# The second edge sweep's sums kept feature by node, on top of the node's own row, and read as they are by the output layer

## The chip, the cores and the metric

One core of a Trainium2 chip runs the whole program in one launch. The metric is the device time of an execution in microseconds; the kernel before takes 1228.67 us (median of 3 runs, 1228.24 to 1230.1).

## The reference

The program computes two graph layers with a residual and a layer norm behind each. There are 1250 nodes with 512 features and 20000 edges, sorted by one end. All of it is fp32.

```python
x = layernorm(x + attention_layer(x))               # first sweep over the edges
# second layer
pre = irrep_linear(x)                               # p0 (128) and p1 (3 x 128)
s0  = [p0[dst], p0[dst], sum_m p1[dst]*p1[src]/3]
g   = silu([x0, |x1|] @ W_g1 + b_g1) @ W_g2 + b_g2
x'  = irrep_linear([g0, x1*g1])                     # the node's own row, 512 wide
w1..w4 = (ssp(edge_attr @ W_f1) @ W_f2) * (ssp(s0 @ W_s1) @ W_s2)
out0 = w1*x0'[src]*sh0 + w4*sum_m x1'[src]*sh1/sqrt(3)
out1 = w2*x0'[src]*sh1 + w3*x1'[src]*sh0
out  = segment_sum([out0, out1], dst) + x'          # sums over edges, plus the own row
out  = [out0 @ W_o0 + b_o0, out1 @ W_o1]            # output layer, per 128-wide part
x    = layernorm(x + out + x)
```

## The kernel before, in words

The nodes are padded to 1280 and stand in `NB` = 10 blocks of `P` = 128. The edges are sorted into `NG` = 88 groups of 256 slots; a group belongs to one block of nodes and is worked on as two halves of 128 edges (`k` = 0, 1). Every engine runs its own instruction list in the order in which `pipelined` (L565) and its short form `pairs` (L584) call the steps: a step with lag n does in iteration i the work of group (or pair of blocks) i - n. Nothing reorders them. Semaphores join the engines. Each `nc.Block()` is a stage; all engines meet at its end.

The stages are: sorting the edges and loading them into slots; the first sweep (L590 on); the node stage (L763 on), which takes the ten blocks in five pairs; the second sweep (L1001 on), 88 groups; and the output stage (L1246 on), again five pairs of blocks.

**The node stage.** For a pair q, VectorE makes the normed row `x1c` (`residual`, `norm`), TensorE turns it (`turn_x`, L888) into PSUM `psX`, ScalarE copies that to `xT` (`x_out`, L841). From `xT` come the squares (`squares`, L803 to L807), `pre` (L896, L899), the gate (`gate1` L906 and L907, `gate_hidden` L859, `gate2` L922, `gate_out` L869, `gated` L820) and the new row (`new_x`, L929 and L931). VectorE's `table_row` (L828, L829) writes it to `tabrow`, raises `row_ready`, and SyncE stores `tabrow` to the table in DRAM that the second sweep gathers from. `keep_self` (L875) is a ScalarE copy of `tabrow` into `selfx`. After the last pair's `residual`, GpSimd clears the accumulator `acc` (L951).

**The second sweep.** For each half k of a group, VectorE has made the messages `mm_sb` (edges on the partitions, 768 wide: 512 for the own components, then 128 and 128 more), a one-hot `oh` of the target node, and `ohs[.., 0..3, :]`, the one-hot scaled by each of the four spherical components (ScalarE makes 1 to 3). TensorE's `sums` adds them up in the PSUM bank `psA`. The one-hot is the stationary operand and the messages move, so `psA` is node by feature:

```python
pe.matmul(psA, ohs[:, u, k, 0, :], mm_sb[:, u, k, 0:D], start=(k == 0), stop=False)      # 512 columns
for m in range(3):                                                                       # 3 x 128 columns
    pe.matmul(psA[:, P*(m+1):P*(m+2)], ohs[:, u, k, m+1, :], mm_sb[:, u, k, D:D+P], start=False, stop=False)
mm = pe.matmul(psA[:, 0:P], oh[:, u, k, :], mm_sb[:, u, k, D+P:D+2*P], start=False, stop=(k == 1))
```

VectorE's `accumulate` (L1197) adds `psA` to the block's rows of `acc`. TensorE's order in one iteration is `inner` (L1055), `sums(0)`, `hidden` (L1082, L1084), `sums(1)`, `sources` (L1096), `factors` (L1109).

**The output stage.** For a pair q: GpSimd adds `acc` and `selfx` into `ya` (`with_self`, L1304); TensorE turns `ya` (`turn_sums`, L1314) into `psY`; ScalarE copies it to `yT` (`sums_out`, L1290); TensorE multiplies it by `W_o0` and `W_o1` into `psO` (`layer`, L1322); VectorE makes the residual `hb` (`residuals`, L1253 and L1255), adds `psO` (`add_layer`, L1260 and L1263), takes the statistics (L1268, L1273), ScalarE the square root (L1294), VectorE the reciprocal and the normed row (`norm`, L1278 and L1282), and SyncE stores it (L1331). `psO` has one buffer: `layer(q)` waits until `add_layer(q - 1)` is done.

Of the kernel before, what the change touches and what calls it, by code (L numbers as in the profile page):

```python
# [8 lines left out]
ALU = mybir.AluOpType  # L9
# [5 lines left out]
P = 128  # L15
# [26 lines left out]
def build(nc, x, src, dst, edge_rows, W, b, a, W_pre0, b_pre0, W_pre1, W_nd0, b_nd0, W_nd1, W_g1, b_g1,  # L42
          W_g2, b_g2, W_f1, W_f2, W_s1, W_s2, W_o0, b_o0, W_o1, out):
    ctx = ExitStack()
    with ctx:
# [710 lines left out]
        xn_ready = sem("xn_ready")  # L756
        row_ready = sem("row_ready")
        self_ready = sem("self_ready")
        tab_out = sem("tab_out")
# [3 lines left out]
        with nc.Block() as block:  # L763
# [69 lines left out]
            def _(act):  # L833
# [38 lines left out]
                def keep_self(q):  # L872

                    act.wait_ge(row_ready, q + 1)
                    act.activation(selfx[:, bass.ds(q * 2, 2), :], tabrow[:, :, 0:D], ACT.Copy).then_inc(self_ready, 1)  # L875
                pairs(act, (1, lengths), (1, p0_out), (1, gate_hidden), (2, keep_self), (0, deviation), (1, part_out),
# [3 lines left out]
            def _(pe):  # L880
                def turn_x(q):

                    pe.wait_ge(x1_ready, q + 1)
                    after(pe, xT_ready, q)
                    for c in range(4):
                        for k in range(2):
                            s_ = x1c[:, k, 0:P] if c == 0 else x1c[:, k, P + c - 1:D:3]
                            mm = pe.transpose(psX[:, c // 2, GE * (c % 2) + P * k:GE * (c % 2) + P * k + P], s_, ident[:, :])  # L888
                    mm.then_inc(xtr_ready, 1)
# [35 lines left out]
                def new_x(q):  # L925
# [6 lines left out]
                    mm.then_inc(xn_ready, 1)  # L932
                pairs(pe, (1, pre), (1, gate1), (1, part), (1, gate2), (0, turn_x), (1, new_x))

# [8 lines left out]
            @block.gpsimd  # L943
            def _(gp):
                def keep_x1(q):
                    gp.wait_ge(x1_ready, q + 1)
                    gp.tensor_copy(x1[:, bass.ds(q * 2, 2), :], x1c[:, :, :]).then_inc(x1_copied, 1)
                pairs(gp, (0, keep_x1))

                gp.wait_ge(hb_ready, NB // 2)  # L950
                gp.memset(acc[:, :, :], 0.0)  # L951

# [48 lines left out]
        with nc.Block() as block:  # L1001
# [45 lines left out]
            def _(pe):  # L1047
# [11 lines left out]
                def sums(k):  # L1059
                    def step(g, c, n):  # L1060
                        u = c % 2
                        if k == 0:
# [3 lines left out]
                            after(pe, acc2_done, g)  # L1066
                        pe.matmul(psA, ohs[:, u, k, 0, :], mm_sb[:, u, k, 0:D], start=(k == 0), stop=False)  # L1067
                        for m in range(3):
                            pe.matmul(psA[:, P * (m + 1):P * (m + 2)], ohs[:, u, k, m + 1, :], mm_sb[:, u, k, D:D + P],  # L1069
                                      start=False, stop=False)  # L1070
                        mm = pe.matmul(psA[:, 0:P], oh[:, u, k, :], mm_sb[:, u, k, D + P:D + 2 * P], start=False, stop=(k == 1))  # L1071
                        if k == 1:
# [150 lines left out]
        sweep2.close()  # L1223
        ya = sb("ya2", [P, 2, D])
        yT = sb("yT2", [P, 2, D])
        hb = sb("hb2", [P, 2, D])
# [4 lines left out]
        outrow = sb("outrow", [P, 2, D])  # L1231
        oa_ready = sem("oa_ready")
        oaT_ready = sem("oaT_ready")
        oT_ready = sem("oT_ready")
        ow_ready = sem("ow_ready")
# [8 lines left out]

        psY, psO = ps[:, 0:2, :], ps[:, 2:4, :]
        with nc.Block() as block:  # L1246
# [40 lines left out]
            def _(act):  # L1287
                def sums_out(q):
                    act.wait_ge(oaT_ready, q + 1)
                    act.activation(yT[:, :, :], psY, ACT.Copy).then_inc(oT_ready, 1)  # L1290

                def deviation(q):
                    act.wait_ge(omv_ready, q + 1)
                    act.activation(sd_[:, :], mv[:, :, 1], ACT.Sqrt, bias=epsc[:, 0:1]).then_inc(osd_ready, 1)  # L1294
                act.preload_act_table_set("sqrt_and_others")
                pairs(act, (0, sums_out), (1, deviation))

            @block.gpsimd
            def _(gp):
                def with_self(q):  # L1300

                    two = bass.ds(q * 2, 2)
                    after(gp, oaT_ready, q)
                    gp.tensor_tensor(ya[:, :, :], acc[:, two, 0:D], selfx[:, two, :], ALU.add).then_inc(oa_ready, 1)  # L1304
                pairs(gp, (0, with_self))

            @block.tensor
            def _(pe):
                def turn_sums(q):
                    pe.wait_ge(oa_ready, q + 1)  # L1310
                    after(pe, oT_ready, q)
                    for k in range(2):
                        for c in range(4):
                            mm = pe.transpose(psY[:, k, P * c:P * c + P], ya[:, k, P * c:P * c + P], ident[:, :])  # L1314
                    mm.then_inc(oaT_ready, 1)

                def layer(q):
                    pe.wait_ge(oT_ready, q + 1)
                    after(pe, oh_done, q)
                    for k in range(2):  # L1320
                        for c in range(4):
                            mm = pe.matmul(psO[:, k, P * c:P * c + P], yT[:, k, P * c:P * c + P],  # L1322
                                           (wo1 if c else wo0)[:, :], start=True, stop=True)
                    mm.then_inc(ow_ready, 1)
                pairs(pe, (0, turn_sums), (0, layer))

# [33 lines left out]
```

## Time and profile before

| | |
|---|---|
| median of 3 runs | 1228.67 us (1228.24 to 1230.1) |
| the profiled execution's own time | 1229.83 us |
| its span in the trace | 1228.1 us |
| TensorE (matmul) busy | 995.1 us, 81% of the span |
| VectorE busy | 854.4 us, 70% |
| GpSimd busy | 780.0 us, 64% |
| ScalarE busy | 533.3 us, 43% |
| node stage | from about 469 to 550 us of the span |
| second sweep | from about 550 to 1185 us |
| output stage | from about 1185 us to the end |

The busy time of TensorE comes from matmuls whose ends are modelled; where one follows another, the start to start distance tells what it costs. An fp32 matmul stands in the trace as two instructions of the same size, each with a weight load of its own; a transpose of an fp32 tile as one. A row of the timeline may merge several equal instructions in a row (x6) into one. The granted clock of TensorE is given as a share of 2.4 GHz, so 0.50 is 1.2 GHz.

### The profile page before, as it was taken

To read this page: it belongs to the slowest core of one execution; us is meant where nothing else is said; L and a number is where in the kernel's file an instruction comes from. 1 tells how busy PE (TensorE), PEld (TensorE's weight loads), DVE (VectorE), ACT (ScalarE), POOL (GpSimd) and SP (SyncE) were. 2 spreads that over 40 slices of the span, in tenths; PEclk is the share of its full clock that TensorE was granted. 3 is DMA by queue.
4 is the path that set the end of the run, shared out by engine and by line. 5 is a ranking of instruction groups with operands and counts; after the bars stand their busy time and mean duration, and the time that the engine had idled before them with its cause. 6 is when DMAs were issued, how large, how long until landed. Compare 5 with 4: busy or idle time off the path is not lost. (4 is left out here: it accounts for less than half of the span.)

```text
span 1228.1 us, 23671 instructions
## 1 busy us (share of the span) xinstructions
PE 995.1 (81%) x5530; PEld 642.5 (52%) x5531; DVE 854.4 (70%) x2190; ACT 533.3 (43%) x1559; POOL 780.0 (64%) x809
## 2 busy tenths in 40 slices
PE   2316556199999996756999999999999999999974
PEld 1213232055555554643666666666666666666653
DVE  7351101177778775744888888888888888888857
ACT  2203121023222333543665666656566555666631
POOL 3777777577777760116676776767667676676721
PEclk9757668699999997886999999999999999999987
DMA  9201011277877780125545545455454555545302
GB/s 346 76 15 33 25 32 50 75 238 238 242 240 241 240 218 17 60 94 180 171 156 165 163 153 171 150 167 161 157 170 148 170 159 159 166 150 167 127 1 86
DMA packets 109167, 177.46 MB, mean 145 GB/s; under 512 B 40191, under 2 KB 79343, under 8 KB 109009
## 3 DMA queue, kind: packets, MB, share of 16 engines
q0 software_dynamic: 33184, 130.15, 33.5%
q1 hardware_dynamic: 72752, 45.60, 12.4%
q10 hardware_dynamic: 3200, 1.38, 0.5%
q8 instruction: 11, 0.18, 0.1%
q14 instruction: 20, 0.16, 0.0%
HBM read 157.31 MB, written 19.74 MB: 144 GB/s over the span
## 5 line engine op out<-in xcount | busy, mean ns | idle before, releaser
L1038 POOL TENSOR_TENSOR dot<-ring,ed 128x768 f32<-128x768 f32 x88 | 129.6, 1473 | 134.1 <-issue 109.8
L698 PE MATMUL ps<-ring,aw 128*128 128x512 f32 x352 | 195.6, 643 | 17.7 <-DVE aw L649 16.3
L1028 POOL DMA_INDIRECT ring<-tab_d,ed x176 | 170.4, 968 | 62.2 <-issue 30.5
L618 POOL DMA_INDIRECT ring<-xt_d,ed x176 | 167.5, 952 | 61.4 <-issue 42.0
L375 POOL DMA_INDIRECT slots_d<-stage,stage_pos x157 | 153.5, 978 | 66.3 <-issue 48.7
L1067 PE MATMUL ps<-mm_sb,ohs 128*128 128x512 f32 x352 | 189.1, 619 | 1.4 <-DVE acc L1197 1.4
L1069 PEld LDWEIGHTS ps<-mm_sb,ohs 128*128 128x128 f32 x1056 | 145.6, 191 | 84.2 <-issue 84.2
L1122 ACT ACTIVATE ohs<-oh,ed 128x128 f32<-128x128 f32 x528 | 172.6, 394 | 0.0
L1152 ACT ACTIVATE S_sb<-ps 128x512 f32<-128x512 f32 x176 | 95.5, 595 | 134.6 <-PE ps L1109 134.6
L1069 PE MATMUL ps<-mm_sb,ohs 128*128 128x128 f32 x1056 | 146.2, 275 | 0.0
L1175 DVE TENSOR_TENSOR ps<-S_sb,ps 128x1024 f32<-128x1024 f32 x88 | 108.2, 1229 | 28.0 <-ACT S_sb L1152 26.8
L699 PEld LDWEIGHTS ps<-ring,aw 128*128 128x128 f32 x352 | 67.5, 192 | 85.7 <-issue 85.7
L1055 PEld LDWEIGHTS ps<-ident,prod 128*128 128x128 f32 x528 | 57.1, 142 | 86.2 <-DVE prod L1165 76.1
L1109 PE MATMUL ps<-w,hcat 32*128 32x512 f32 x704 | 101.3, 645 | 0.8 <-DVE hcat L1170 0.8
L1197 DVE TENSOR_TENSOR acc<-acc,ps 128x512 f32 x88 | 60.6, 688 | 45.7 <-PE ps L1071 45.7
L661 DVE TENSOR_TENSOR acc<-acc,ps 128x513 f32 x88 | 60.7, 690 | 43.1 <-issue 30.1
L1055 PE MATMUL ps<-ident,prod 128*128 128x128 f32 x528 | 78.0, 285 | 13.3 <-DVE prod L1165 12.0
L1165 DVE TENSOR_TENSOR prod<-ps,ring 128x768 f32<-128x768 f32 x88 | 83.6, 950 | 6.8 <-DMA ring<-tab_d,ed 6.8
L1185 DVE TENSOR_TENSOR mm_sb<-ps,ring 128x768 f32<-128x768 f32 x88 | 83.3, 946 | 0.0
L1096 PE MATMUL ps<-p1h,ohT 128*128 x176 | 67.7, 385 | 10.3 <-DVE ohT L1216 10.0
L284 DVE CAST stage<-loc_i 128x16 f32<-128x16 int32 (+1 forms) x10 | 1.8, 182 | 105.0 <-DMA slots_d<-stage,stage_pos 104.9
L630 DVE SCALAR_TENSOR_TENSOR junk<-iota,ed,srow 128x128 f32<-128x128 f32 x176 | 54.9, 348 | 24.7 <-DMA ed<-slots_d 18.5
(194 smaller groups left out, 1859.0 us busy)
## 6 DMA issues: line engine op xcount, KB each, us to landing
ilb<-f_d SPq DMA_DIRECT2D x88, 128.0 KB, 3.8
ed<-slots_d SPq DMA_DIRECT2D x176, 38.0 KB, 3.8
tab_d<-tabrow SPq DMA_DIRECT2D x5, 896.0 KB, 3.7
slots_d<-fill SPq DMA_DIRECT2D x8, 418.0 KB, 4.3
f_d<-ft SPq DMA_DIRECT2D x88, 38.0 KB
ring<-xt_d,ed POOLq DMA_INDIRECT x176, 4.0
hcat<-f_d SPq DMA_DIRECT2D x176, 16.0 KB, 3.8
ring<-tab_d,ed POOLq DMA_INDIRECT x176, 4.4
```

Source lines behind the costliest of these rows:

```text
L375: g.indirect_dma_start(slots_d[:, :], bass.IndirectOffsetOnAxis(ap=stage_pos[:, h, k:k + 1], axis=0), stage[:, h, k, :], None).then_inc(sc ...
L618: gp.indirect_dma_start(xg[:, c, k, :], None, xt_d[:, :], bass.IndirectOffsetOnAxis(ap=ed[:, c, k, JD:JD + 1].bitcast(I32), axis=0))\
L698: pe.matmul(ps[:, 2 * u, :], aw[:, r, k, :], xg[:, c, k, 0:D], start=(k == 0), stop=(k == 1))
L1028: gp.indirect_dma_start(xj[:, r, k, :], None, tab_d[:, :], bass.IndirectOffsetOnAxis(ap=ed[:, c, k, JD:JD + 1].bitcast(I32), axis=0))\
L1038: gp.tensor_tensor(dot[:, u, :, :, :], xj[:, r, :, P:D].rearrange("p k (m n) -> p k m n", m=3), ed[:, c, :, IL + 2:IL + 5].unsqueeze(3).to ...
L1055: mm = pe.matmul(psI[:, P * k:P * k + P], prod[:, k, P * m:P * m + P], ident[:, :], is_transpose=True, start=(m == 0), stop=(m == 2))
L1067: pe.matmul(psA, ohs[:, u, k, 0, :], mm_sb[:, u, k, 0:D], start=(k == 0), stop=False)
L1069: pe.matmul(psA[:, P * (m + 1):P * (m + 2)], ohs[:, u, k, m + 1, :], mm_sb[:, u, k, D:D + P], start=False, stop=False)
L1109: mm = pe.matmul((psS if q < 2 else psF)[:, q % 2, :], hcat[rows, c, :], w2[rows, :], start=True, stop=True)
L1122: ins = act.activation(ohs[:, u, k, m, :], oh[:, u, k, :], ACT.Copy, scale=ed[:, c, k, IL + 1 + m:IL + 2 + m])
L1152: ins = act.activation(S_sb[:, k, :], psS[:, k, :], ACT.Copy)
L1175: v.tensor_tensor(psF, S_sb[:, :, :], psF, ALU.mult).then_inc(w_done, 1)
```

## The change

In the second sweep, the messages become the stationary operand and the one-hots move, so that `psA`, and with it `acc`, are feature by node within each block of 128 by 128. For one half of a group the 512-wide matmul becomes four of 128 columns (one for each 128 features), and the three of 128 columns that shared the message part `mm_sb[.., D:D+P]` become one of 384 columns. In the node stage TensorE turns the new row (`turn_self`) into `psX` as soon as it is in `tabrow`, and ScalarE's `keep_self` copies it from there into `acc`, rearranged, in place of the copy into `selfx`; GpSimd no longer clears `acc`. `psX` is shared with `turn_x`, which now waits for `keep_self` of the pair that was turned before. In the output stage the GpSimd addition, the turn and the ScalarE copy are gone, and `layer` takes `acc` as its stationary operand.

```diff
@@ node stage
                 def keep_self(q):
-                    act.wait_ge(row_ready, q + 1)
-                    act.activation(selfx[:, bass.ds(q * 2, 2), :], tabrow[:, :, 0:D], ACT.Copy).then_inc(self_ready, 1)
+                    act.wait_ge(self_turned, q + 1)
+                    act.activation(acc[:, bass.ds(q * 2, 2), 0:D].rearrange("p k (c n) -> p c k n", n=P),
+                                   psX.rearrange("p a b -> p (a b)").rearrange("p (c k n) -> p c k n", c=4, k=2), ACT.Copy).then_inc(self_ready, 1)
@@
                     pe.wait_ge(x1_ready, q + 1)
                     after(pe, xT_ready, q)
+                    after(pe, self_ready, q - 1)
                     for c in range(4):
@@
-                pairs(pe, (1, pre), (1, gate1), (1, part), (1, gate2), (0, turn_x), (1, new_x))
+
+                def turn_self(q):
+
+                    pe.wait_ge(row_ready, q + 1)
+                    for c in range(4):
+                        for k in range(2):
+                            mm = pe.transpose(psX[:, c // 2, GE * (c % 2) + P * k:GE * (c % 2) + P * k + P],
+                                              tabrow[:, k, P * c:P * c + P], ident[:, :])
+                    mm.then_inc(self_turned, 1)
+                pairs(pe, (1, pre), (2, turn_self), (1, gate1), (1, part), (1, gate2), (0, turn_x), (1, new_x))
@@
                 pairs(gp, (0, keep_x1))
-
-                gp.wait_ge(hb_ready, NB // 2)
-                gp.memset(acc[:, :, :], 0.0)
@@ second sweep
-                        pe.matmul(psA, ohs[:, u, k, 0, :], mm_sb[:, u, k, 0:D], start=(k == 0), stop=False)
-                        for m in range(3):
-                            pe.matmul(psA[:, P * (m + 1):P * (m + 2)], ohs[:, u, k, m + 1, :], mm_sb[:, u, k, D:D + P],
-                                      start=False, stop=False)
-                        mm = pe.matmul(psA[:, 0:P], oh[:, u, k, :], mm_sb[:, u, k, D + P:D + 2 * P], start=False, stop=(k == 1))
+                        for m in range(4):
+                            pe.matmul(psA[:, P * m:P * m + P], mm_sb[:, u, k, P * m:P * m + P], ohs[:, u, k, 0, :],
+                                      start=(k == 0 and m == 0), stop=False)
+                        pe.matmul(psA[:, P:D], mm_sb[:, u, k, D:D + P], ohs[:, u, k, 1:4, :].rearrange("p m n -> p (m n)"), start=False, stop=False)
+                        mm = pe.matmul(psA[:, 0:P], mm_sb[:, u, k, D + P:D + 2 * P], oh[:, u, k, :], start=False, stop=(k == 1))
@@ output stage
-        psY, psO = ps[:, 0:2, :], ps[:, 2:4, :]
+        psO = ps[:, 0:2, :]
@@ scalar
-                def sums_out(q):
-                    act.wait_ge(oaT_ready, q + 1)
-                    act.activation(yT[:, :, :], psY, ACT.Copy).then_inc(oT_ready, 1)
...
-                pairs(act, (0, sums_out), (1, deviation))
-
-            @block.gpsimd
-            def _(gp):
-                def with_self(q):
-
-                    two = bass.ds(q * 2, 2)
-                    after(gp, oaT_ready, q)
-                    gp.tensor_tensor(ya[:, :, :], acc[:, two, 0:D], selfx[:, two, :], ALU.add).then_inc(oa_ready, 1)
-                pairs(gp, (0, with_self))
+                pairs(act, (0, deviation))
@@ tensor
-                def turn_sums(q):
-                    pe.wait_ge(oa_ready, q + 1)
-                    after(pe, oT_ready, q)
-                    for k in range(2):
-                        for c in range(4):
-                            mm = pe.transpose(psY[:, k, P * c:P * c + P], ya[:, k, P * c:P * c + P], ident[:, :])
-                    mm.then_inc(oaT_ready, 1)
-
                 def layer(q):
-                    pe.wait_ge(oT_ready, q + 1)
                     after(pe, oh_done, q)
                     for k in range(2):
                         for c in range(4):
-                            mm = pe.matmul(psO[:, k, P * c:P * c + P], yT[:, k, P * c:P * c + P],
+                            mm = pe.matmul(psO[:, k, P * c:P * c + P],
+                                           acc[:, q * 2 + k, P * c:P * c + P],
                                            (wo1 if c else wo0)[:, :], start=True, stop=True)
                     mm.then_inc(ow_ready, 1)
-                pairs(pe, (0, turn_sums), (0, layer))
+                for q in range(NB // 2):
+                    layer(q)
```

TensorE's list in the loop of the node stage, before (`x1c` is the normed row, `xT` the turned one, `n1T` the lengths, `hT` the hidden gate):

```order
L896 MATMUL ps<-xT,wpre 128x256
L899 MATMUL ps<-wpre,xT 128x128 x6
L906 MATMUL ps<-xT,wg 128x256
L907 MATMUL ps<-n1T,wg 128x256
...
L914 MATMUL ps<-ws1ab,p0T 128x32 x2
L922 MATMUL ps<-hT,wg 128x256 x4
...
L888 MATMUL ps<-ident,x1c 128x128 x8
```

And with the change, where L899, L902, L909, L910, L917, L925 and L891 are the same steps under their new line numbers:

```order
L899 MATMUL ps<-xT,wpre 128x256
L902 MATMUL ps<-wpre,xT 128x128 x6
L942 MATMUL ps<-ident,tabrow 128x128 x8
L909 MATMUL ps<-xT,wg 128x256
L910 MATMUL ps<-n1T,wg 128x256
...
L917 MATMUL ps<-ws1ab,p0T 128x32 x2
L925 MATMUL ps<-hT,wg 128x256 x4
...
L891 MATMUL ps<-ident,x1c 128x128 x8
```

The eight transposes of the row from two iterations back (L942) now stand between `pre` and `gate1`, so `gate1` and all behind it on TensorE are queued behind their wait for `row_ready`.

## Rows read from the trace of the kernel before

**Rows 1.** Windows by stage: busy us of each engine (instructions), granted clock share, DMA
```profile
700.00:900.00 200.00, 197.91 (x1320) 130.45 (x1319) 175.13 (x345) 120.93 (x373) 139.12 (x143) 1.00 0.51 162
...
1185.00:1228.10 43.10, 20.68 (x120) 19.11 (x120) 28.71 (x60) 7.88 (x11) 11.15 (x5) 0.72 0.16 62
```

**Rows 2.** Timeline of TensorE, second sweep, one group: start us, us busy
```profile
800.56 1.02 PE L1067 MATMUL ps<-mm_sb,ohs 128*128 128x512 f32 x2
801.42 0.83 PE L1069 MATMUL ps<-mm_sb,ohs 128*128 128x128 f32 x6
802.09 0.39 PE L1071 MATMUL ps<-mm_sb,oh 128*128 128x128 f32 x2
...
802.97 1.12 PE L1067 MATMUL ps<-mm_sb,ohs 128*128 128x512 f32 x2
...
807.49 1.02 PE L1067 MATMUL ps<-mm_sb,ohs 128*128 128x512 f32 x2
```

**Rows 3.** Line L1067 over the whole run: weight loads (ns), idle before them (us, times)
```profile
L1067 PEld LDWEIGHTS ps<-mm_sb,ohs x352: 186/190/192, 577.4 to 1182.1; 128*128 128x128 f32 x176
...
  issue: 17.8, 87
```

**Rows 4.** Timeline, node stage, from one normed row to the next
```profile
489.12 1.13 PE L888 MATMUL ps<-ident,x1c 128*128 128x128 f32 x8 [1.37 <-DVE x1c L797]
...
494.00 0.60 PE L906 MATMUL ps<-xT,wg 128*128 128x256 f32 x2
494.09 0.41 DVE L829 TENSOR_TENSOR tabrow<-ps,bnd_bc 128x256 f32<-128x256 f32 x1
...
495.99 0.84 ACT L859 ACTIVATE hT<-ps,bg 128x256 f32<-128x256 f32 x2
...
496.71 1.05 ACT L875 ACTIVATE xt<-tabrow 128x1024 f32 x1
...
497.79 1.28 ACT L836 ACT_TABLE_LOAD   x1
...
500.19 0.29 ACT L836 ACTIVATE sd_<-mv,epsc 128x2 f32<-128x2 f32 x1 [1.11 <-DVE mv L786]
...
501.77 1.97 PE L888 MATMUL ps<-ident,x1c 128*128 128x128 f32 x8 [2.90 <-DVE x1c L797]
```

**Rows 5.** Timeline, end of the node stage and first rows of the next
```profile
534.59 0.41 DVE L829 TENSOR_TENSOR tabrow<-ps,bnd_bc 128x256 f32<-128x256 f32 x1
534.70 0.30 PEld L906 LDWEIGHTS ps<-xT,wg 128*128 128x128 f32 x2
...
545.82 0.41 DVE L829 TENSOR_TENSOR tabrow<-ps,bnd_bc 128x256 f32<-128x256 f32 x1
...
550.51 0.37 SPq L1010 DMA_DIRECT2D ed<-slots_d  x1
```

**Rows 6.** Timeline, output stage, first two pairs of blocks
```profile
1185.12 2.33 POOL L1304 TENSOR_TENSOR ya<-acc,xt 128x1024 f32<-128x1024 f32 x1 [12.10 <-POOLq L1001]
...
1187.51 1.97 PE L1314 MATMUL ps<-ident,ya 128*128 128x128 f32 x8 [3.53 <-POOL ya L1304]
...
1190.59 3.71 PE L1322 MATMUL ps<-wo,yT 128*128 128x128 f32 x16 [1.11 <-ACT yT L1290]
...
1194.42 0.42 DVE L1260 TENSOR_TENSOR hb<-hb,ps 128x256 f32<-128x256 f32 x1 [6.21 <-PE ps L1322]
...
1199.66 2.35 DVE L1255 TENSOR_SCALAR hb<-x 128x768 f32 x1
1202.05 0.42 DVE L1260 TENSOR_TENSOR hb<-hb,ps 128x256 f32<-128x256 f32 x1
```

**Rows 7.** Timeline, output stage, a later pair
```profile
1213.93 0.42 DVE L1260 TENSOR_TENSOR hb<-hb,ps 128x256 f32<-128x256 f32 x1
...
1215.42 3.75 PE L1322 MATMUL ps<-wo,yT 128*128 128x128 f32 x16 [3.04 <-DVE hb L1263]
...
1219.86 0.42 DVE L1260 TENSOR_TENSOR hb<-hb,ps 128x256 f32<-128x256 f32 x1
```

More of the change, by code:

```diff
@@ L757, in build @@
         row_ready = sem("row_ready")
+        self_turned = sem("self_turned")
         self_ready = sem("self_ready")
@@ L1223, in build @@
         sweep2.close()
-        ya = sb("ya2", [P, 2, D])
-        yT = sb("yT2", [P, 2, D])
         hb = sb("hb2", [P, 2, D])
@@ L1231, in build @@
         outrow = sb("outrow", [P, 2, D])
-        oa_ready = sem("oa_ready")
-        oaT_ready = sem("oaT_ready")
-        oT_ready = sem("oT_ready")
         ow_ready = sem("ow_ready")
```

## The prediction, made before the changed kernel ran

> **What bounds the kernel now.** I read the windows by stage first, then the timeline of one group of the second sweep, then the timelines of the node stage and of the output stage. In the middle of the second sweep TensorE is busy for 197.91 of 200 us at the full granted clock, VectorE for 175 and GpSimd for 139 [rows 1]: every nanosecond added to TensorE's list there counts 88 times, and nothing on another engine does. One group takes 6.93 us, from the 512-wide matmul at 800.56 to the next group's at 807.49 [rows 2], and 88 of them are half of the run. In the output stage no engine is full (20.68 us of matmul and 28.71 of VectorE in 43.1 [rows 1]): a chain of waits sets its time. The node stage is a chain of that kind too.
>
> **Output stage: removed.** The first pair of blocks goes through GpSimd (2.33 us), a turn (1.97), a ScalarE copy, and the layer (3.71), and VectorE adds the layer at 1194.42 after 6.21 us idle [rows 6]. With the change `layer` needs only `acc`, which is complete when the stage begins. It can start where GpSimd did, at about 1185.2. Its 16 instructions of 128 columns take 16 x 0.112 = 1.8 us at the high clock (0.67 us from 801.42 to 802.09 for six [rows 2]) plus some 0.2 for the last one's way out. VectorE adds at about 1187.3: a gain of 7.1. At the low clock it is the 3.71 of the row, and the gain is 5.4. I take the high one: TensorE's last matmul of the sweep ends at 1187.51 - 3.53 = 1183.98 [rows 6], 1.2 us before, and a turn that followed 1.37 us of idleness took 1.13 us where one after 2.90 us took 1.97 [rows 4], which are the two levels, 2.4 and 1.2 GHz.
>
> Second, VectorE's scale of the residual takes 2.35 us at 1199.66, beside a GpSimd addition, where the same line later in the stage does 0.55. From the first L1260 to the second it is 7.63 us [rows 6], and later 5.93 (1213.93 to 1219.86 [rows 7]). GpSimd has no work left in the stage, so each pair has the later period: a gain of 1.7. The first pair's slow residual hid under the chain and would now show; it goes too. What is late next is VectorE's own chain: add, statistics, root, norm, residual. `layer` lies under it: even at the low clock it starts at 1215.42, when the add before is done, and takes 3.75 us, to 1219.17, and VectorE comes to it at 1219.86 [rows 7]. The margin is 0.7 us; the removed turns and copies were not on this path in the later pairs. Sum of the stage: **-8.8 us**, with ends -7.1 (first layer cold) and -8.8.
>
> **Node stage: added.** The turn (8 transposes) stands ahead of `gate1` on TensorE and waits for `tabrow`. In the iteration of rows 4 `gate1` starts at 494.00, and `tabrow` is complete at 494.09 + 0.41 = 494.50. The turn then takes 8 x 0.11 = 0.9 us at the high clock, so with 0.1 us for the semaphore `gate1` starts at 495.5, 1.5 us later. Behind it wait `part` and `gate2`, and on ScalarE `gate_hidden`, which moves from 495.99 to 497.5, then `keep_self` (1.05 us, from PSUM now; the same size of copy, so the same price) to about 499.25, and the table load (1.28 us) to 500.57. ScalarE's root came at 500.19 before, where ScalarE had been idle for 1.11 us, waiting for VectorE [rows 4]. So 1.1 of the 1.5 us lie in that idleness and 0.4 remain. It is the same in the iterations of pairs 2, 3 and 4: +1.1 us. In the iteration behind the last pair VectorE has no new rows to norm, and the gate's chain is itself the path. There the row before is complete at 535.00 and the first weight load of `gate1` was at 534.70 [rows 5]: with the turn it comes at 536.0, +1.3 us. The last turn and copy cost some 2.2 us, 3.3 at the low clock. They lie beside the store of the table row: from 546.23, when the row is complete, to 550.51, when the second sweep's first load is issued, there are 4.3 us [rows 5]. Nothing for them, as long as those 4.3 stand.
>
> The same delay may give something back. `gate2` ends 1.5 us later and the next `turn_x` comes 0.4 us later, so TensorE's idle time ahead of it shrinks from 2.90 to about 1.8 us, which is nearer to the 1.37 after which the turn took 1.13 us than to the 2.90 after which it took 1.97 [rows 4]. The slow one stands in each of the three iterations that hold a turn of `tabrow` and a `turn_x`, and the turn is on the path (copy, squares and all of VectorE's list are behind it). I take two of the three at the high clock: -1.7 us. The wait of `turn_x` for `keep_self` costs nothing: the copy ends at 499.25, the turn starts at about 502. The GpSimd clearing of `acc` goes; it lay beside the last pair's chain and nobody waited for it: 0. Sum of the stage: **+0.7 us**. If all three turns are fast it is -0.1; if none is, +2.4; if the four added turns in the loop and behind it run at the low clock as well (0.84 us more each), +5.8.
>
> **Second sweep: changed.** The columns stay the same: 512 + 4 x 128 = 1024 for one half of a group before, 5 x 128 + 384 = 1024 now. Instructions go from 10 to 12 (each matmul is two). Price of one by its columns, start to start: 512 columns take 0.43 us (800.56 to 801.42 for two), 128 take 0.112 [rows 2]. That is 0.83 ns a column and 5 to 6 ns an instruction; 384 columns then take 0.324. One half: 0.86 + 8 x 0.1117 = 1.754 before, 10 x 0.1117 + 2 x 0.324 = 1.765 now, that is +0.011 us; 176 halves: **+2.0 us**. The starts are read to 0.01 us, so this could be 0 to 4. This holds if a weight load hides under a matmul of 128 columns. Six with a load each (0.19 us of load, 186 to 192 ns [rows 3]) came at 0.112 each [rows 2], so it does for eight in a row; the change makes a row of fourteen of them, with `inner`'s six transposes ahead. A load that isn't hidden can be seen too: ahead of the second half's first matmul the weight load waits (17.8 us in 87 times [rows 3]), and that pair is busy for 1.12 us where the first half's is for 1.02 [rows 2]. It costs 0.10, and stays as it is, once in a group. The upper bound is all 352 added loads at that price, 35 us. What the instructions wait for doesn't change, nor do VectorE's additions of `psA`.
>
> The Trainium skill speaks against this part: "TensorE: Matmul & The Clock Gate", section Back-to-back issue gap, gives for a stream of load and matmul pairs some 81 ns at 128 columns and 131 at 512, so that small ones cost far more by the column. By that, four passes of fp32 in each half, and a 384-wide one put between the two, I estimate 4 x (193 - 129) = 256 ns for a half and 45 us in all. The trace disagrees for this kernel: its 512-wide instruction takes 3.8 times the 128-wide one's distance, not 1.6.
>
> **Sum.** -8.8 + 0.7 + 2.0 = -6.1 us. Against the profiled execution's own 1229.83 that is 1223.7. The median of the runs shown is 1.2 lower, so the forecast is 1222.6.
>
> **The rivals.**
> *Exposed weight loads (slower).* In the row of fourteen 128-wide instructions in the second sweep the weight loads fall behind, since no 512-wide one lets them catch up. For it: a load lasts 0.19 us and a new one is due every 0.11. Against it: the eight in a row that keep their pace, and that the clock of the whole sweep is set by columns. Price: up to 0.10 us for each of 352, which gives 1228.7 - 8.1 + 35 = 1256. It decides the sign from 23 ns for each added instruction on (8.1 / 352). Chance 0.08.
> *The node stage takes it all back.* All added turns and all `turn_x` run at the low clock (+5.8) and the first layer of the output stage too (-7.1); with +2.0 in the sweep that is +0.7, or 1229.4. For it: the granted clock falls often in that stage, and the turn does go cold after 2.90 us. Against it: more of TensorE's time is filled, not less. The whole of it is unlikely, half of it gives 1226. Chance 0.09 for within 0.2%.
> *Everything goes well.* All three `turn_x` are fast (-0.1), the sweep costs nothing because the three matmuls that are merged save as much as the four cost: -8.9, or 1219.8. It is on the forecast's side. Chance 0.2.
> *The forecast*, 1221 to 1226: chance 0.63.
>
> **How the numbers follow.** A measurement of this kernel can tell 0.2% (2.5 us) from no change. The forecast and the good case are faster by more than that: 0.83. Within 0.2%: 0.09. Slower: 0.08. The range holds the good case with 2 us below it for the reading of the starts in the sweep, and reaches up to where half of the rival in the node stage lies, with the upper reading of the sweep (+4): 1218 to 1228. The exposed loads are left out of it.
>
> **What would show each step.** The sweep: the distance from one group to the next, 6.93 before, 6.95 if I am right, 7.3 with exposed loads; the line of the four 128-wide ones at 0.11 each. The output stage: VectorE's first add of the layer some 2.3 us behind the stage's start in place of 9.3, and 5.93 from one pair to the next throughout, with L1253 and L1255 never above 0.6 us. The node stage: `gate1` behind the turn, ScalarE's idle time ahead of the root gone, the duration of `turn_x` 1.13 or 1.97. The forecast is wrong if a group takes over 6.97 us, or if the node stage takes over 3 us more.

## The result, and the profile after

The changed kernel takes 1223.04 us (median of 5 runs, 1221.94 to 1227.11), the kernel before on the same chip 1228.74 (1228.24 to 1230.1). The ratio is 0.9957 with a 95% interval of 0.9939 to 0.9975: 5.7 us less by the medians, 5.3 by the ratio. Forecast were 1222.6 and -6.1.

The profiled execution is the slowest of the five (1227.11 us, span 1225.4), so its span is only 2.7 us below that of before. Laid side by side, the starts of the same instructions give the account:

| piece (start to start) | before | after | difference | forecast |
|---|---|---|---|---|
| up to the node stage's first instruction | 469.83 | 471.38 | +1.55 | 0 |
| node stage, to the last row's last write | 75.99 | 79.04 | +3.05 | +0.7 |
| from there to the sweep's first sum | 31.73 | 32.21 | +0.48 | 0 |
| sweep, first sum to last addition | 606.57 | 607.73 | +1.16 | +2.0 |
| last addition to the output stage's first | 1.01 | 1.02 | 0 | 0 |
| output stage, to the first addition of the layer | 9.29 | 2.13 | -7.16 | -7.1 |
| first to fifth addition of the layer | 25.44 | 23.65 | -1.79 | -1.7 |

The program up to the node stage is the same in both kernels. In the 14 profiles of this case that stage begins between 469.8 and 472.8 us, and the kernel before happens to hold the lowest: the 1.55 us aren't the change's. Nor can the 0.48 us be put down to it: from the last row's last write to the sweep's first sum it is 29.71 to 33.41 us in the 14 profiles, and 29.71 and 31.66 in two of one and the same kernel. The node stage's +3.05 is just past the 3 us that the prediction named as a sign of being wrong; the second profile of the same kernel, below, has -0.80.

The timeline of the output stage after (start us, us busy, idle before) answers to [rows 6, 7]:

```profile
1191.38 2.02 PE L1304 MATMUL ps<-wo,acc 128*128 128x128 f32 x16 [1.16 <-PEq L1010]
1191.38 0.43 DVE L1257 SCALAR_TENSOR_TENSOR hb<-x,bo_bc 128x256 f32<-128x256 f32 x1 [0.32 <-PEq L1010]
...
1193.51 0.42 DVE L1264 TENSOR_TENSOR hb<-hb,ps 128x256 f32<-128x256 f32 x1 [1.24 <-PE ps L1304]
...
1198.77 0.55 DVE L1259 TENSOR_SCALAR hb<-x 128x768 f32 x1
1199.35 0.42 DVE L1264 TENSOR_TENSOR hb<-hb,ps 128x256 f32<-128x256 f32 x1
...
1212.63 3.79 PE L1304 MATMUL ps<-wo,acc 128*128 128x128 f32 x16 [2.15 <-DVE hb L1267]
...
1217.16 0.42 DVE L1264 TENSOR_TENSOR hb<-hb,ps 128x256 f32<-128x256 f32 x1
```

The layer starts with the stage and runs at the high clock (2.02 us). VectorE waits 1.24 us for it and not 6.21. Its scale of the residual takes 0.55 us where it took 2.35. Later the layer falls to the low clock (3.79 us) and still ends at 1216.42, ahead of VectorE's 1217.16: the margin that the prediction put at 0.7 us.

The timeline of TensorE over one group of the second sweep after, to be laid beside [rows 2]:

```profile
799.18 1.06 PE L1077 MATMUL ps<-ohs,mm_sb 128*128 128x128 f32 x8
800.08 0.81 PE L1079 MATMUL ps<-ohs,mm_sb 128*128 128x384 f32 x2
800.72 0.38 PE L1080 MATMUL ps<-oh,mm_sb 128*128 128x128 f32 x2
...
806.12 1.06 PE L1077 MATMUL ps<-ohs,mm_sb 128*128 128x128 f32 x8
```

Eight of 128 columns in 0.90 us are 0.112 each, with `inner`'s six ahead of them; two of 384 take 0.64. The group takes 6.94 us for 6.93.

The timeline of the node stage after, one iteration, answers to [rows 4]:

```profile
504.52 1.44 PE L891 MATMUL ps<-ident,x1c 128*128 128x128 f32 x8 [2.00 <-DVE x1c L798]
505.75 0.64 PE L932 MATMUL ps<-wnd,gT 128*128 128x128 f32 x2
506.18 1.49 PE L934 MATMUL ps<-wnd,xgT 128*128 128x128 f32 x6
...
510.12 0.41 DVE L830 TENSOR_TENSOR tabrow<-ps,bnd_bc 128x256 f32<-128x256 f32 x1
510.66 1.04 PE L942 MATMUL ps<-ident,tabrow 128*128 128x128 f32 x8
...
510.99 0.96 DVE L814 TENSOR_SCALAR p1h<-ps 128x768 f32 x1 [0.45 <-PE ps L902]
...
516.75 0.29 ACT L837 ACTIVATE sd_<-mv,epsc 128x2 f32<-128x2 f32 x1 [0.23 <-DVE mv L787]
```

`gate1` stands behind the turn, as forecast. ScalarE's idle time ahead of the root shrank from 1.11 to 0.23 us and did not vanish, so it was not ScalarE that ended the iteration: VectorE had waited 0.45 us for `pre` (L814). And `pre` was late because `new_x` (L932, L934), ahead of it on TensorE, ran at the low clock: 1.49 us for six instructions. The turn of the normed row took 1.44 us, part of it at either clock.

### The profile page after: what moved, and what is told of

The parts are those of the page before. It is cut to its first block and busy times, and to the rows that moved or that the text cites. A ratio compares the mean times of both kernels' runs of the same rounds, so it can differ in the third digit from the quotient of the medians.

```text
span 1225.4 us, 24314 instructions
## 1 busy us (share of the span) xinstructions
PE 997.7 (81%) x5882; PEld 682.9 (56%) x5883; DVE 851.2 (69%) x2190; ACT 527.1 (43%) x1554; POOL 767.1 (63%) x803
## 3 DMA queue, kind: packets, MB, share of 16 engines
q10 hardware_dynamic: 3200, 1.38, 0.5%
## 5 line engine op out<-in xcount | busy, mean ns | idle before, releaser
L1077 PE MATMUL ps<-ohs,mm_sb 128*128 128x128 f32 x1408 | 194.9, 281 | 1.4 <-DVE acc L1206 1.4
L1077 PEld LDWEIGHTS ps<-ohs,mm_sb 128*128 128x128 f32 x1408 | 170.7, 191 | 19.3 <-issue 17.8
L1079 PE MATMUL ps<-ohs,mm_sb 128*128 128x384 f32 x352 | 142.7, 487 | 0.0
L1184 DVE TENSOR_TENSOR ps<-S_sb,ps 128x1024 f32<-128x1024 f32 x88 | 108.2, 1229 | 28.6 <-ACT S_sb L1161 27.3
L1080 PEld LDWEIGHTS ps<-oh,mm_sb 128*128 128x128 f32 x352 | 66.9, 190 | 46.6
```

The costliest lines, as they stand in the source:

```text
L1077: pe.matmul(psA[:, P * m:P * m + P], mm_sb[:, u, k, P * m:P * m + P], ohs[:, u, k, 0, :], start=(k == 0 and m == 0), stop=False)
L1079: pe.matmul(psA[:, P:D], mm_sb[:, u, k, D:D + P], ohs[:, u, k, 1:4, :].rearrange("p m n -> p (m n)"), start=False, stop=False)
L1184: v.tensor_tensor(psF, S_sb[:, :, :], psF, ALU.mult).then_inc(w_done, 1)
```

## The experiments

Theory: the output stage gives 8.9 us by its two mechanisms; the sweep's loss is a few ns for each added instruction; the node stage loses by the turn's place, and its length moves by more than that with TensorE's clock. Rivals: weight loads that fall behind in the sweep; a node stage whose 3 us are all the change's own, or all the clock's. Times on one chip are compared; lengths of stages come from each run's profile and are compared across chips.

**One part alone: the sweep.** In the kernel before, only this:

```diff
-                        pe.matmul(psA, ohs[:, u, k, 0, :], mm_sb[:, u, k, 0:D], start=(k == 0), stop=False)
-                        for m in range(3): ...
+                        for m in range(4):
+                            pe.matmul(psA[:, P*m:P*m+P], mm_sb[:, u, k, P*m:P*m+P], ohs[:, u, k, 0, :], ...)
+                        pe.matmul(psA[:, P:D], mm_sb[:, u, k, D:D+P], ohs[:, u, k, 1:4, :]..., ...)
```

> The kernel before with only the second sweep's matmuls turned (messages stationary, one-hots moving); the node and output stages are as before, so the rows that are summed up and the own row no longer have the same layout, and the output isn't the reference's. Theory (an fp32 instruction costs 5 to 6 ns beside its columns): +1 to +2 us against the kernel before, one group 6.94 us. Rival (weight loads of the 128-wide instructions fall behind): +8 us or more, and first-line instructions over 0.12 us apart.

1231.6 us against 1230.18 for the kernel before, ratio 1.0017 (1.0003 to 1.0031): +1.4 us by the medians. The sweep takes 607.74 us.

**The rest without the sweep.** In the changed kernel, the reverse of that diff.

> The changed kernel with the second sweep's matmuls as before (one-hots stationary); node and output stages as changed; the sums are then in the other layout than the own row, and the output isn't the reference's. Theory: 1 to 2 us faster than the changed kernel, some 7 us faster than the kernel before. If weight loads were exposed: over 8 us faster than the changed kernel.

1221.22 us, ratio 0.9928 (0.9911 to 0.9944) on the same chip, 9.0 us below the kernel before where I expected 7. The sweep takes 606.85 us. From one profile to the other the sweep hardly moves: 606.57, 606.62 and 606.85 us in the three with the old form, 607.63 to 607.74 in nine of the ten with the new one (608.21 in the tenth). So the turned sweep costs 1.0 us, half of the forecast 2.0.

**Three narrow ones for the wide one.** In the changed kernel:

```diff
-                        pe.matmul(psA[:, P:D], mm_sb[:, u, k, D:D + P], ohs[:, u, k, 1:4, :].rearrange("p m n -> p (m n)"), start=False, stop=False)
+                        for m in range(1, 4):
+                            pe.matmul(psA[:, P * m:P * m + P], mm_sb[:, u, k, D:D + P], ohs[:, u, k, m, :], start=False, stop=False)
```

> The changed kernel with the 384-wide matmul taken apart into three of 128 columns with the same stationary operand: 352 + 352 more instructions and weight loads in the sweep, the same columns. Theory (3 to 6 ns for an instruction): sweep 609.7 to 611.7 us, 2 to 4 us slower than the changed kernel. Rival (in a longer row of 128-wide ones the weight loads fall behind): over 10 us slower.

1225.49 us against 1221.75 for the changed kernel on the same chip. The sweep takes 610.68 us, 3.0 more for 704 added instructions, each with a weight load: 4.3 ns each. The timeline of TensorE there:

```profile
803.11 0.87 PE L1064 MATMUL ps<-ident,prod 128*128 128x128 f32 x6
803.82 1.06 PE L1077 MATMUL ps<-ohs,mm_sb 128*128 128x128 f32 x8
804.72 0.83 PE L1080 MATMUL ps<-ohs,mm_sb 128*128 128x128 f32 x6
805.38 0.39 PE L1081 MATMUL ps<-oh,mm_sb 128*128 128x128 f32 x2
```

Twenty-two instructions of 128 columns follow one another from `inner`'s six at 803.11 on, and the six of L1080 are 0.110 us apart like those before. No load falls behind; the rival, that they would, is out.

**A GpSimd addition beside the residual.** In the changed kernel's output stage, read by nobody:

```diff
...
+            @block.gpsimd
+            def _(gp):
+                def with_self(q):
+                    two = bass.ds(q * 2, 2)
+                    after(gp, orow_ready, q)
+                    after(gp, oa_ready, q)
+                    gp.tensor_tensor(ya[:, :, :], acc[:, two, 0:D], selfx[:, two, :], ALU.add).then_inc(oa_ready, 1)
+                pairs(gp, (0, with_self))
```

> The changed kernel with a GpSimd addition of acc and x (read by nobody) in the output stage, started for each pair when the pair before is normed, so beside VectorE's scale of the residual. Theory (the addition holds VectorE's SBUF-only instructions up, 2.35 us for 0.55): each of the four later pairs about 1.8 us longer, first addition of the layer about 1 us later, output stage 8 us longer. Rival (the 2.35 us came from something else in the old chain): no change.

```profile
1191.52 2.35 POOL L1307 TENSOR_TENSOR ya<-acc,xt 128x1024 f32<-128x1024 f32 x1 [12.14 <-POOLq L1010]
1191.53 2.61 DVE L1259 SCALAR_TENSOR_TENSOR hb<-x,bo_bc 128x256 f32<-128x256 f32 x1 [0.32 <-PEq L1010]
...
1199.69 2.15 POOL L1307 TENSOR_TENSOR ya<-acc,xt 128x1024 f32 x1 [5.82 <-DVE outrow L1288]
1199.90 2.35 DVE L1261 TENSOR_SCALAR hb<-x 128x768 f32 x1
1202.29 0.42 DVE L1266 TENSOR_TENSOR hb<-hb,ps 128x256 f32<-128x256 f32 x1
```

The 2.61 and 2.35 us are back, each ending just behind the GpSimd instruction beside it. The first addition of the layer comes 3.12 us behind the stage's start for 2.13, and the first to the fifth take 31.52 us for 23.65: 7.9 us, 2.0 a pair. In two of the four later pairs the scale takes 2.35 or 2.36 us and the pair is 1.80 us longer, in the other two it takes 2.69 and the pair is 2.14 longer: the excess over 0.55 us, to 0.01. The time is 1230.27, 8.7 us above the 1221.59 of the changed kernel with eight unread transposes in its node stage (below), the nearest kernel run on that chip. That it equals the kernel before (1230.18) is a coincidence: there only one later pair has a slow scale, but also the chain ahead of the first layer. The 1.8 us term of the output stage is this mechanism, and the kernel before with unread transposes, below, shows it from the other side.

**Without the turn.** In the changed kernel:

```diff
-                    act.wait_ge(self_turned, q + 1)
-                    act.activation(acc[:, bass.ds(q * 2, 2), 0:D].rearrange(...), psX..., ACT.Copy).then_inc(self_ready, 1)
+                    act.wait_ge(row_ready, q + 1)
+                    act.activation(acc[:, bass.ds(q * 2, 2), 0:D], tabrow[:, :, 0:D], ACT.Copy).then_inc(self_ready, 1)
...
-                pairs(pe, (1, pre), (2, turn_self), (1, gate1), (1, part), (1, gate2), (0, turn_x), (1, new_x))
+                pairs(pe, (1, pre), (1, gate1), (1, part), (1, gate2), (0, turn_x), (1, new_x))
```

> The changed kernel without the turn of the own row: ScalarE copies it from tabrow into acc unturned, and turn_x waits for nothing new. The own row is in the wrong layout, so the output isn't the reference's. Theory (the turn costs the node stage 1.3 us in its last iteration and 0.3 in each before, and the rest is the clock's luck): 2 to 3 us faster than the changed kernel; the stage ends 1.3 us or more earlier. Rival (the node stage's loss is the clock alone, not the wait): no faster than the changed kernel.

1222.9 us, ratio to the kernel before 0.9942 (0.9926 to 0.9958), with nothing to be seen of the 2 to 3 us that I expected: the changed kernel, which wasn't run on that chip, has the same ratio on another (next run). The node stage takes 76.71 us: one iteration, in which `turn_x` and all of `new_x` fell to the low clock, took 15.03 us where the one before took 12.64. This run alone doesn't tell the theories apart.

**The changed kernel again.**

> The changed kernel once more, for a second profile and on the chip of this call. Theory (the node stage's length follows TensorE's clock, which falls at another place from run to run, while the other stages are fixed): sweep from first sum to last addition 607.7 us again, output stage the same to 0.05 us, node stage somewhere between 75.8 and 79 us; time 5 to 7 us below the kernel before. Rival (the node stage's 79.0 us of the first profile is the change's own): 79 us again.

1221.75 us beside 1229.97 for the kernel before, ratio 0.9942 (0.9927 to 0.9957): 8.2 us less by the medians, 7.1 by the ratio, where I expected 5 to 7. The same program's node stage takes 75.19 us this time, 3.85 less than in its first profile. The other pieces stand where they were (sweep 607.65, output stage 2.13 and 23.65). The timeline of TensorE, the same iteration as shown above:

```profile
504.19 1.12 PE L891 MATMUL ps<-ident,x1c 128*128 128x128 f32 x8 [1.78 <-DVE x1c L798]
505.15 0.40 PE L932 MATMUL ps<-wnd,gT 128*128 128x128 f32 x2
505.38 0.83 PE L934 MATMUL ps<-wnd,xgT 128*128 128x128 f32 x6
```

And the end of that iteration, on ScalarE and VectorE:

```profile
514.27 1.28 ACT L837 ACT_TABLE_LOAD   x1
515.56 0.29 ACT L837 ACTIVATE sd_<-mv,epsc 128x2 f32<-128x2 f32 x1
515.89 0.17 DVE L792 RECIPROCAL rstd<-sd_ 128x2 f32<-128x2 f32 x1 [0.69 <-ACT sd_ L837]
```

ScalarE's idle time ahead of the root is gone: the root follows its table load at once, and VectorE waits 0.69 us for it, where in the first profile it waits 0.36. So with the clock high it is ScalarE that ends the iteration, 0.33 us late, as the prediction had it; the wait for `pre` belongs to the iterations in which the clock fell.

Between the two it is the granted clock that differs: from 490 to 505 us it is 1.00 here and 0.89 in the first profile. These are the windows of TensorE's and the other engines' busy time over that stretch, first of the first profile, then of the second (the last three columns are the granted clock, the DMA share and GB/s):

```profile
490.00:505.00 15.00, 11.77 (x70) 10.84 (x71) 11.39 (x22) 8.30 (x14) 1.91 (x2) 0.89 0.16 62
505.00:520.00 15.00, 12.45 (x74) 11.53 (x73) 10.56 (x20) 8.12 (x14) 2.77 (x2) 0.85 0.15 61
```

```profile
490.00:505.00 15.00, 10.92 (x73) 9.65 (x74) 12.04 (x23) 8.84 (x16) 2.23 (x2) 1.00 0.16 62
505.00:520.00 15.00, 12.15 (x85) 10.75 (x84) 10.59 (x21) 9.76 (x15) 2.48 (x2) 1.00 0.15 61
```

**The turn behind `gate2`.** In the changed kernel, with `psN` as its target and ScalarE's copy behind `gate_out`:

```diff
-                pairs(pe, (1, pre), (2, turn_self), (1, gate1), (1, part), (1, gate2), (0, turn_x), (1, new_x))
+                pairs(pe, (1, pre), (1, gate1), (1, part), (1, gate2), (2, turn_self), (0, turn_x), (1, new_x))
```

> The changed kernel with the turn of the own row moved behind gate2 on TensorE, into psN (free between table_row and new_x), and ScalarE's copy of it behind gate_out; turn_x doesn't wait for it, new_x does. Theory (what costs is the place ahead of gate1): as fast as without the turn, 1.5 to 3 us faster than the changed kernel, gate1 right behind pre again. Rival (TensorE's time for it costs wherever it stands): same as the changed kernel.

> The kernel with the turn behind gate2, once more and beside the changed kernel on one chip. Theory: its last iteration is 2 to 3 us shorter than the changed kernel's, its time 1 to 3 us less. Rival: no difference.

1221.92 us on the first chip (0.9939, 0.992 to 0.9957), 1222.09 on the second, beside 1221.75 of the changed kernel: no gain that can be measured, against what I expected. The node stage takes 74.14 us in one profile, where two of the four later turns of the normed row are fast (1.12 and 1.13 us), and 76.74 in the other, where all four took 1.48 to 1.90. By the medians alone the turn's place would have passed for free. The next runs take the clock out.

**Transposes that nobody reads.** Ahead of each `turn_x`, in the kernel with the late turn, in the changed kernel (there behind the wait for `self_ready`), and in the kernel before:

```diff
+                def fill(q):
+                    for c in range(8):
+                        pe.transpose(psX[:, 0, 0:P], ident[:, :], ident[:, :])
-                pairs(pe, ..., (1, gate2), (2, turn_self), (0, turn_x), (1, new_x))
+                pairs(pe, ..., (1, gate2), (2, turn_self), (0, fill), (0, turn_x), (1, new_x))
```

> The kernel with the late turn, and eight transposes that nobody reads ahead of each turn of the normed row, while TensorE waits for it. Theory (what varies in the node stage is the clock that falls in TensorE's idle time): the turns of the later pairs take 1.13 us each, new_x stays at the high clock, node stage 74 us or less. Rival (the clock is not what stretches the stage): as the late turn without them, or slower by what they take.

> The changed kernel, its turn ahead of gate1 as it is, with the eight unread transposes ahead of each turn of the normed row. Theory (the turn's place costs 0.3 us an iteration and 1.3 in the last, the clock the rest): node stage 74 to 74.5 us, against 72.0 with the late turn and the same transposes; 2 us slower than that one. Rival (all of the change's node stage loss is the clock): 72 us.

> The kernel before with the eight unread transposes ahead of each turn of the normed row. Theory (TensorE's clock falls in its idle time there too: three of five turns took 1.97 us): the later turns 1.13 us, node stage 72 to 73 us for 76, time 2 to 4 us less than the kernel before. Rival (only the changed kernel has something to gain): same as before.

With the late turn 1219.79 us, beside 1222.09 without the fill; the stage takes 72.0 us, and all four later turns of the normed row 1.13 or 1.14. With the changed kernel's own place the stage takes 73.78. In both, the clock stays high from the second pair on. That gives the price of the place at one clock: 12.98, 12.96 and 12.97 us from one normed row to the next against 12.66, 12.64 and 12.65, so 0.32 in each of three iterations; and 17.03 against 15.83 us from the last normed row to the last write of the table, so 1.2. I had 0.38 and 1.3. The time of that kernel, 1221.59 us (0.9947, 0.9931 to 0.9962), shows no gain by the transposes: without them the ratio was 0.9942, on another chip, and in its second profile all four later turns were fast anyway.

In the kernel before, the expectation for the node stage failed. The last two turns took 1.27 and 1.42 us and the stage 75.98, as without the transposes; the turn at 502.85 took 1.12 us, but six instructions of `new_x` behind it took 1.49, and the iteration 13.82. The time is 1227.8 for 1230.18 (0.9987, 0.9975 to 1.0). What is shorter in the profile is the output stage, which is the same code as before:

```profile
1188.89 1.09 PE L1318 MATMUL ps<-ident,ya 128*128 128x128 f32 x8 [3.53 <-POOL ya L1308]
...
1200.46 0.55 DVE L1259 TENSOR_SCALAR hb<-x 128x768 f32 x1
1200.90 1.99 POOL L1308 TENSOR_TENSOR ya<-acc,xt 128x1024 f32 x1 [1.69 <-PE ps L1318]
1201.05 0.42 DVE L1264 TENSOR_TENSOR hb<-hb,ps 128x256 f32<-128x256 f32 x1
```

The first turn is at the high clock here, behind the same 3.53 us of idleness as in [rows 6], and the GpSimd addition starts behind VectorE's scale and not ahead of it: the scale takes 0.55 us and not 2.35. To the first addition of the layer it is 8.48 us, and 23.86 from there to the fifth, together 2.4 us less than in the profile of before (9.29 and 25.44). Whether the transposes in the node stage have a part in that, one profile can't tell.

**Filling the first idle time too.** The same with 32 transposes ahead of the first turn:

> The late turn with the unread transposes, and 32 of them ahead of the first turn too, where TensorE is idle for 5 us and the first pair's work all runs at 1.2 GHz. Theory: the first iteration, 14.0 us from one normed row to the next, drops to 12.7 and the stage to some 70.5 us. Rival (the transposes run at the low clock and end later than the normed row is there): no gain or a loss of 1 to 2 us.

1217.47 us, ratio 0.9911 (0.9894 to 0.9928), the fastest of all, 4.1 us below the changed kernel with its own place and the eight transposes on that chip (1221.59). The timeline and the windows of that run at the start of the node stage:

```profile
470.81 3.69 PE L948 MATMUL ps<-ident 128*128 128x128 f32 x32 [1.16 <-PEq L590]
...
476.07 1.13 PE L890 MATMUL ps<-ident,x1c 128*128 128x128 f32 x8 [1.58 <-DVE x1c L798]
```

```profile
470.00:475.00 5.00, 3.69 (x32) 3.48 (x32) 3.93 (x10) 1.58 (x2) 0.00 (x0) 1.00 0.00 0
475.00:480.00 5.00, 2.82 (x21) 2.58 (x22) 2.64 (x5) 1.02 (x1) 1.03 (x1) 1.00 0.01 3
480.00:485.00 5.00, 4.12 (x23) 3.45 (x22) 4.53 (x9) 4.18 (x6) 0.00 (x0) 1.00 0.00 0
```

The clock of the sweep before was still high and stayed so. In the run with the late turn and eight in that place it was 0.84, 0.50 and 0.63 in the same windows, and the first turn took 1.97 us, behind 4.20 us of idleness for 1.58 here. The two runs differ in both, the transposes and the idleness behind them, and nothing tells the two apart. The first iteration drops from 14.02 to 11.44 us, the stage to 69.41.

## Why the prediction was right

The forecast was 1222.6 with 1218 to 1228, faster with a chance of 0.83; 1223.04 is measured. The terms are right or nearly so, each by its mechanism, but the node stage's has luck in it and the output stage's depends on the profile it was read from.

*Output stage*, -8.8 with ends -7.1 and -8.8: -7.16 - 1.79 = -8.95. Both steps hold to 0.1 us, and so does the choice of the high clock for the first layer: it took 2.02 us in all eleven profiles with the new output stage. The ground that I gave, 1.2 us of idleness where a turn behind 1.37 us had been fast, doesn't carry that far: behind the same 1.38 us the last turn of the own row took 1.09 us in the first profile of the changed kernel and 1.97 in the second. What I did not see is that the stage before is not fixed either. The unread transposes ahead of `turn_x` leave its code alone, and there it is 2.4 us shorter; against that profile the gain would be 6.6 us. The one that I predicted from and that of the sweep alone have the longer course (34.7 us to the fifth addition, for 32.3); how often each comes isn't known.

*Second sweep*, +2.0: +1.0 in all comparisons. The mechanism was right and the term twice too large. The step that was off is "0.83 ns a column and 5 to 6 ns an instruction", drawn from two starts read to 0.01 us; the runs show 352 instructions for 1.0 us, 3 ns each, and 704 for 3.0 us, 4.3 each. The bound that I gave for it (0 to 4 us) held.

*Exposed weight loads*, the rival with 0.08: refuted by the sweep alone (+1.4 us in the time and 1.0 in the sweep, where the rival had up to 35) and by twice as many added loads (3 us). The rule that I quoted beside it, some 81 ns at 128 columns and 131 at 512 ("TensorE: Matmul & The Clock Gate", Back-to-back issue gap of the Trainium skill), does not hold for this stream. One fp32 instruction of 128 columns takes 0.112 us with its load under it, in rows of fourteen and twenty-two, and its time goes by its columns.

*Node stage*, +0.7 with ends -0.1 and +5.8: between -0.8 and +3.05 in the five profiles with the changed kernel's node code (75.19, 75.59, 75.78, 79.00 and 79.04 us, against 75.99), +0.9 on average. The parts that I could read from rows were right, 0.38 an iteration (0.32 to 0.33) and 1.3 at the end (1.2). The mechanism too: in the second profile, with the clock high, it is ScalarE's table load that holds the root back. The part "two of the three at the high clock" was a guess at something that the program doesn't fix. The same code had all of them fast in three profiles, and in two had all four spread over 1.27 to 1.72 us with `new_x` slow behind them. I had put the clock's effect on the turns alone, and as one of two durations; the first profile shows it on `new_x` and through it on `pre` and on VectorE's reading of it (L814). That wait, and not the table load, ended the iteration there. The end of -0.1 was off: with the four later turns of the normed row fast the stage was 0.2 to 0.8 us shorter than before.

*No cost for the last turn and copy beside the store of the table*: right. From the last write of the table row to the sweep's first load it is 4.70 us after and 4.69 before, and in the second profile of the changed kernel 4.69 with that turn at the low clock.

## What to carry to other kernels

When stages differ in what bounds them, price the change by stage and lay the starts of the same instructions side by side afterwards: a chain of three engines ahead of a first result was worth 7 us of 1229, while 704 more instructions with the same columns on the engine that bounds the kernel cost 3. A profile of one execution can hide or invent 2 to 4 us in a stage where TensorE is often idle, in the kernel before as in the changed one; profile the same kernel twice before you explain such a difference. If the clock matters there, TensorE's idle time is a place to try work that nobody reads, and to measure it: with the late turn, 64 transposes brought the node stage from 74.1 and 76.7 us to 69.4 and the ratio to the kernel before from 0.9939 to 0.9911, some 3.4 us. Eight a turn gave nothing that can be measured in the changed kernel, and at most 0.25% in the kernel before.

## What the runs showed of the hardware that I had not expected

The high clock outlasts a run of transposes of an identity: with 32 of them in 3.69 us, and 1.58 us of idleness behind, it stayed at 1.00; with 8, and 4.20 us of idleness, it fell to 0.50. The length of the idleness alone doesn't tell the clock: the turn behind 1.38 us of it took 1.09 us in one profile and 1.97 in another of the same program, and that behind 3.53 us took 1.97 us in two profiles and 1.09 in a third.

The same program's node stage varies by 3.85 us with where the clock falls, while the sweep of 607 us, in which TensorE is hardly ever idle, varies by 0.3 from one profile to the next (0.6 in one case). The new output stage, without the added GpSimd work, takes the same to 0.02 us in ten profiles. The old one doesn't: where its first turn was 0.88 us faster, a GpSimd addition missed VectorE's scale, which was worth another 1.6 us.
